# Splitting the raw down weights for the first fold stage, two heads without partial sums, and earlier maxima and gain loads

## The reference, cut to what matters

```python
h = _layernorm(x) * (1 + ca) + sa
scores = einsum('bqhd,bkd->bhqk', q, k) / HEAD_DIM ** 0.5      # causal
attn = softmax(scores)
x = x + ga * (einsum('bhqk,bkd->bqhd', attn, v) @ o_w.T + o_b)
h = _layernorm(x) * (1 + cb) + sb
y = fwht(h * SU_ug) / SCALE
y = silu(y @ W_gate.T * ws_gate) * (y @ W_up.T * ws_up)
y = fwht(y * SU_dp) / SCALE
x = x + gb * (y @ W_down.T * ws_down)
```

## Time and profile before

| | us |
|---|---|
| median of the runs | 1907.4 (1904.89 to 1908.88) |
| the profiled execution | 1910.14 |
| its span, first to last instruction | 1907.9 |
| PE busy | 1853.8 (97%) |
| DVE busy | 1368.3 (72%) |
| ACT busy | 848.6 (44%) |
| GpSimd busy | 555.2 (29%) |

### The profile page before, as it was taken

The page is one execution under the profiler, slowest core; times in us unless marked ns, Lnnn a source line. Parts: engine busy times, 40 slices in busy tenths (PEclk is TensorE's granted clock), DMA queues, the critical chain, the costliest instruction groups (busy, mean ns, idle before and its releaser), DMA issues.

```text
span 1907.9 us, 37938 instructions
## 1 busy us (share of the span) xinstructions
PE 1853.8 (97%) x14016; PEld 1554.0 (81%) x14016; DVE 1368.3 (72%) x3223; ACT 848.6 (44%) x1591; POOL 555.2 (29%) x653
## 2 busy tenths in 40 slices
PE   6999999999999999889999999999999999999998
PEld 3677777777777777668887889999999999999997
DVE  4788887878787777845558886776777666767655
ACT  4368655766576645642224433323323333333221
POOL 2367676667665655640100010100100100001000
PEclk8799999999999999989999999999999999999999
DMA  7433334343435778444459887888797787888884
GB/s 235 135 103 80 107 101 119 93 108 99 127 85 148 220 231 286 149 166 162 143 197 372 327 328 286 298 322 314 291 348 285 290 335 284 310 325 298 322 301 166
DMA packets 118702, 424.47 MB, mean 222 GB/s; under 512 B 26348, under 2 KB 39916, under 8 KB 104312
## 3 DMA queue, kind: packets, MB, share of 16 engines
q1 hardware_dynamic: 106856, 363.27, 55.9%
q10 hardware_dynamic: 11664, 58.79, 8.2%
HBM read 322.36 MB, written 65.29 MB: 203 GB/s over the span
## 4 chain that ended last, share of the span: by engine, by line
PE 47%; DVE 5%; ACT 2%; issue 1%; DMA 1%; POOL 1%; SPq 1%; DVEq 0%; ACTq 0%; POOLq 0%
PE banks L1822 23%; PE banks L1912 15%; PE banks L1691 7%; DVE ln_stats L1265 1%; POOL probs L1120 1%; PE banks L1788 1%; PE banks L1782 1%; DMA upgate_items_dram<-items_ring 1%; DVE x_normed L1277 1%; PE banks L1990 1%; DVE y L1390 0%; DMA upgate_raw<-in_w_ug 0%; ACT silu_gate L919 0%; ACT y_split L904 0%; ACT silu_gate L954 0%
## 5 line engine op out<-in xcount | busy, mean ns | idle before, releaser
L1120 POOL TENSOR_TENSOR probs<-probs 128x512 f32<-128x512 f32 x256 | 340.4, 1330 | 181.7 <-ACT probs L1015 160.5
L1912 PE MATMUL banks<-d_ring,y_split 128*128 128x512 f32 x1536 | 377.4, 392 | 1.9 <-DVE y_split L1410 1.9
L1015 ACT ACTIVATE probs<-banks 128x512 f32<-128x512 f32 x576 | 310.1, 596 | 103.3 <-PE banks L1958 100.0
L1912 PEld LDWEIGHTS banks<-d_ring,y_split 128*128 128x128 f32 x1536 | 281.7, 188 | 56.8 <-DVE y_split L1410 2.1
L1822 PE MATMUL banks<-h_t_split,items_ring 128*128 128x256 f32 x2280 | 321.0, 283 | 2.0 <-DVE both L1367 2.0
L1822 PEld LDWEIGHTS banks<-h_t_split,items_ring 128*128 128x128 f32 x2280 | 299.0, 191 | 13.8 <-ACT h_t L830 4.0
L1958 PE MATMUL banks<-q_stacks,k_stack 98*128 98x512 f32 (+3 forms) x768 | 250.8, 369 | 8.5 <-DMA q_stacks<-neg_max_rows 6.0
L1745 PE MATMUL banks<-k_stack,q_stacks 96*128 96x512 f32 (+3 forms) x768 | 249.9, 369 | 7.0 <-DMA q_stacks<-q_split 2.6
L1822 PE MATMUL banks<-input_sums,items_ring 128*128 128x256 f32 x1710 | 236.2, 283 | 0.0
L1149 POOL TENSOR_TENSOR x_normed<-h_t 128x512 f32<-128x512 f32 x6 | 7.9, 1309 | 775.6 <-ACT h_t L837 775.6
L1822 PEld LDWEIGHTS banks<-input_sums,items_ring 128*128 128x128 f32 x1710 | 218.9, 192 | 0.0
(11 more groups left out here) (180 smaller groups left out, 2612.7 us busy)
## 6 DMA issues: line engine op xcount, KB each, us to landing
items_ring<-upgate_items_dram SPq DMA_DIRECT2D x94, 1792.0 KB, 7.3
d_ring<-down_split_dram SPq DMA_DIRECT2D x128, 512.0 KB, 8.1
q_stacks<-q_split SPq DMA_DIRECT2D x192, 128.0 KB, 2.8
upgate_raw<-in_w_ug SPq DMA_DIRECT2D x32, 512.0 KB, 4.4
upgate_items_dram<-items_ring ACTq DMA_DIRECT2D x8, 1792.0 KB, 7.2
upgate_items_dram<-items_made ACTq DMA_DIRECT2D x8, 1792.0 KB, 6.8
x<-in_x SPq DMA_DIRECT2D x32, 256.0 KB, 2.9
o_group<-o_and_sums SPq DMA_DIRECT2D x256, 32.0 KB
```

The source lines that it names most:

```text
L1015: nc.scalar.activation(pr[:, probs_slot(H, u), :], score_bank[:, at % SLOTS_SCORE, :], ACT.Exp, scale=SCALE).then_inc(exped, 1)
L1120: nc.gpsimd.tensor_tensor(into, into if i else pr[:, probs_slot(H, u - 1), :], pr[:, probs_slot(H, u), :], ALU.add).then_inc(summed, 1)
L1912: last = nc.tensor.matmul(acc[:, t, :], ys[s][:, a, t * P:(t + 1) * P], dr[g % D_RING][:, m, :], start=(f == 0 and a + m == 0), stop=(f == ...
```

## The change

1. **Split raw weights.** ACT rounds a raw down-weight tile to float32r (`raw_high`), DVE takes the rest (`raw_rest`), into a new buffer `fold_raw_split` of two tiles, and the across tile becomes two float32r matmuls. Both are made two across tiles ahead, right behind the split of a tile's product; the first two in H = 46 behind units 0 and 2. The matrix `across` is copied once to float32r.
2. **Places of the across tiles.** Three in H = 48 (units 4, 7, 8) and in H = 52, none in H = 53. The first two along tiles are loaded five units before H = 54 starts, and no more one (`LOAD_BEFORE`).
3. **Two heads without added tiles.** In H = 62 and 63 GpSimd adds nothing, and PE multiplies every probability tile by ones (`WEIGHED_UNSUMMED`).
4. **Maxima of head 1.** Slots 0 to 2 stand before the turn of head 0's maxima, slots 3 to 5 behind the turn of the values, all ahead of head 0's first score; six fewer stand in head 0.
5. **Gains and residuals.** `load_gains` and two `load_residual` of the last batch move from behind the last head into SP's H = 61.
6. **Second block's input.** It is loaded in step 2 of the network, and no more in step 1.
7. Three semaphores of the start become one.

```diff
-FOLDS = [("across", left, u) for left, us in [(left, (4, 8)) for left in range(18, 11, -1)] + [(11, (1, 4))] for u in us]
+FOLDS = [("across", left, u) for left in range(18, 11, -1) for u in ((4, 7, 8) if left in (16, 12) else (4, 8))]
+FIRST_SPLITS = {(18, 0): 0, (18, 2): 1}
-STORE_AFTER, LOAD_BEFORE, FIRST_LOADS = 1, 1, 4
+STORE_AFTER, LOAD_BEFORE, FIRST_LOADS = 1, 5, 4
...
+            def raw_high(i):
+                if i == 0:
+                    act.wait_ge(across_in, 16)
+                    nc.scalar.activation(across[:], across_raw, ACT.Copy)
+                act.wait_ge(fold_in[i % FOLD_RING], 16 * (i // FOLD_RING + 1))
+                nc.scalar.activation(raw_split[:, i % 2, 0, :], raw[:, i % FOLD_RING, :], ACT.Copy).then_inc(raw_hi, 1)
...
                     nc.scalar.activation(fold[:, i % 2, 0, :], side[:, r, :], ACT.Copy).then_inc(fold_hi, 1)
+                    if i + 2 < FT:
+                        raw_high(i + 2)
...
+            def raw_rest(i):
+                dve.wait_ge(raw_hi, i + 1)
+                nc.vector.tensor_tensor(raw_split[:, i % 2, 1, :], raw[:, i % FOLD_RING, :], raw_split[:, i % 2, 0, :].bitcast(F32), ALU.subtract).then_inc(raw_lo, 1)
...
                     nc.vector.tensor_tensor(lo, side[:, r, :], hi.bitcast(F32), ALU.subtract).then_inc(side_free[r], 1)
+                    if i + 2 < FT:
+                        raw_rest(i + 2)
...
-                    pe.wait_ge(across_in, 16)
-                    pe.wait_ge(fold_in[i % FOLD_RING], 16 * (i // FOLD_RING + 1))
+                    pe.wait_ge(raw_lo, i + 1)
                     r = side_slot(key)
-                    last = nc.tensor.matmul(side[:, r, :], across[:], raw[:, i % FOLD_RING, :], start=True, stop=True)
+                    for m in range(2):
+                        last = nc.tensor.matmul(side[:, r, :], across[:], raw_split[:, i % 2, m, :], start=m == 0, stop=m == 1)
...
-                    if u in SUMMED_UNITS:
+                    if u in SUMMED_UNITS and H < ALL - UNSUMMED_HEADS:
                         add_unit(H, u)
...
-    return order + [("max", 0, i) for i in range(NS)] + [("top", 0), ("v", 0)]
+    order += [("max", 0, i) for i in range(NS)] + [("max", 1, i) for i in range(AHEAD_OF_TOP)] + [("top", 0), ("v", 0)]
+    return order + [("max", 1, i) for i in range(AHEAD_OF_TOP, EARLY_MAXIMA)]
...
+                if left == TAIL_IN:
+                    load_gains(B - 1)
+                    for t in range(2):
+                        load_residual(B - 1, t)
```

More of the change, by code:

```diff
@@ L94 @@
 FIRST_TOP_UNIT = 6
+AHEAD_OF_TOP, EARLY_MAXIMA = 3, 6
 SHIFTS_STEP, SHIFTS_UNIT = 1, 4
@@ L174, in side_work @@
     if H == 0:
-        for place, key in enumerate([("max", 1, i) for i in range(NS)] + [("max", 2, i) for i in range(NS)]):
+        for place, key in enumerate([("max", 1, i) for i in range(EARLY_MAXIMA, NS)] + [("max", 2, i) for i in range(NS)]):
             units[place // 2].append(key)
@@ L270, in program @@
                 x1xr=place(s, "x1_and_residual", [P, 4, D]), ga=place(s, "gain_row", [P, D]),
-                ob=place(s, "output_bias", [P, D]), across=place(s, "across", [P, P]),
+                ob=place(s, "output_bias", [P, D]), across=place(s, "across", [P, P], F32R),
                 kvb=place(s, "kvb", [P, 1]), qb=place(s, "qb_group", [P, 1]),
@@ L281, in program @@
                 W["raw"] = place(first, "fold_raw", [P, FOLD_RING, D])
+                W["raw_split"] = place(first, "fold_raw_split", [P, 2, 2, D], F32R)
             W["again"] = place(s, "fold_again", [P, AGAIN_RING, 2, D], F32R)
@@ L378, in phase @@
     x1, xr = x1xr[:, 0:2, :], x1xr[:, 2:4, :]
-    raw, fold, again, across = W["raw"], W["fold"], W["again"], W["across"]
+    raw, raw_split, fold, again, across = W["raw"], W["raw_split"], W["fold"], W["again"], W["across"]
     fx1, xn, hs, hb, fht = F["x1"], F["xn"], F["hs"], F["hb"], F["ht"]
@@ L387, in lent @@
         return buffer[:, first:first + k * n].rearrange("p (k n) -> p k n", k=k)
+    across_raw = fold[:, 1, 1, 0:P].bitcast(F32)
     q_raw, q_split, ow_raw = x1xr[:], Z["q_split"], Z["ow_raw"]
@@ L618, in network @@
                     load_items(g + HALVES_RING - FIRST_HALVES)
-                if f == X_STEP:
+                if f == (X_STEP if blk else FIRST_X_STEP):
                     if blk:
@@ L726, in _ @@
             load_down(2)
-            load_gains(B - 1)
-            for t in range(2):
-                load_residual(B - 1, t)
             for n in range(2):
@@ L783, in load_fold @@
                     if i == 0:
-                        act.dma_start(across[:], io["across"]).then_inc(across_in, 16)
+                        act.dma_start(across_raw, io["across"]).then_inc(across_in, 16)
                     act.dma_start(raw[:, i % FOLD_RING, :], io["w_down"].rearrange("(q j) n -> j q n", j=FT)[i]).then_inc(fold_in[i % FOLD_RING], 16)
@@ L1028, in step @@
                     left = ALL - H
+                    if (left, u) in FIRST_SPLITS:
+                        raw_high(FIRST_SPLITS[left, u])
                     if left == CROSS_LEFT and u == 6:
@@ L1565, in step @@
                     left = ALL - H
+                    if (left, u) in FIRST_SPLITS:
+                        raw_rest(FIRST_SPLITS[left, u])
                     if left == STAT_LEFT and 3 <= u < 3 + NT:
@@ L1980, in weigh @@
                     pe.wait_ge(masked, (H + 1) * len(TRIANGLES))
-                    pe.wait_ge(summed, (H + 1) * len(SUMMED_UNITS))
-                begun, last_of = set(range(PAIRS)) if part else set(), {row: i for i, (row, _, _) in enumerate(WEIGHED[part])}
-                for i, (row, kt, of) in enumerate(WEIGHED[part]):
+                    if H < ALL - UNSUMMED_HEADS:
+                        pe.wait_ge(summed, (H + 1) * len(SUMMED_UNITS))
+                products = (WEIGHED if H < ALL - UNSUMMED_HEADS else WEIGHED_UNSUMMED)[part]
+                begun, last_of = set(range(PAIRS)) if part else set(), {row: i for i, (row, _, _) in enumerate(products)}
+                for i, (row, kt, of) in enumerate(products):
                     if kt == "sum":
```

35 lines of the change are left out of this document (25 added, 10 removed).

## The result

| | before | changed |
|---|---|---|
| median, us | 1907.4 (1903.3 to 1908.9, 5 runs) | 1895.1 (1892.8 to 1899.0, 5 runs) |
| ratio | | 0.9936, interval 0.9919 to 0.9952 |
| the profiled execution | 1910.1 | 1895.1 |
| its span | 1907.9 | 1893.3 |
| PE busy | 1853.8 | 1846.4 |

The changed kernel is faster by 12 us, between the forecast (1899.1) and rival (a) (1893.1), and inside the range. It also lies just inside the forecast's own band, which began at 1894.5. All eleven runs of the changed kernel together have a median of 1894.9.

What follows compares the result with a forecast made beforehand. PE was taken to bound the attention, with DVE becoming the bound of heads 46 to 52. Terms -0.3 - 1.6 - 1.3 - 3.6 - 1.55 = -8.35 us, from median 1907.4, gave 1899.1 us; range 1890.5 to 1907.5.

Steps and rivals of the forecast that it cites:

- rival (a): Heads 46 to 52: no waiting for GpSimd, PE stays the bound; -14.3 us in all, 1893.1 us; chance 18%.
- the forecast's own band: Whole kernel: 1894.5 to 1903.5 us, the span given to the forecast itself, chance 50%.
- First fold stage: Heads 46 to 53: PE saves work on across tiles but DVE becomes the bound of heads 46 to 52; -0.3 us.
- The term of `raw_rest`: DVE, heads 46 to 52: each raw_rest costs 0.62 plus 0.36 us of waiting, 0.98; 16 cost 15.7 us.
- an operation that comes at a random time: First fold stage: raw_rest meets GpSimd's work by chance, waiting 0.33 us for adds and about 0.03 for masks.
- Rival (c): First fold stage: DVE waits for GpSimd at most raw_rest, 1.17 us each; +4.6 us, 1912.0 us; chance 9%.
- Second fold stage: First along tile, head 54: earlier stores and loads remove PE's wait of 1.58 us; -1.6 us.
- Start: Ahead of head 0: six maxima of head 1 fill PE's idle time; -1.3 us, bounds 0 and -3.5.
- if the clock rises when it does now: Start, head 0: with the half clock lasting until near 76 us as before, work done by then counts; -1.3 us.
- Last heads: Heads 62 and 63: GpSimd's waits go, head 63's maxima come later; -3.6 us, between 0 and -6.
- Rival (b): Last head: its maxima come only at 822.8; +2.7 us and not -3.6, 1905.4 us; chance 15%.
- First network steps: Network step 3: up and gate weights issued 2.72 us earlier, so the 1.55 us wait goes; -1.55 us.

Runs made afterwards that it cites:

- the kernel with both corrections: Changed kernel with raw_rest behind unit 8 issued three maxima later and gains and residuals loaded a head later; 1887.9 us, ratio 0.9893 to the kernel before.
- the changed kernel (again): The changed kernel, unchanged, run and profiled a second time beside the experiments; median 1894.0 us, ratio 0.9924 to the kernel before.

## Why the prediction was right, and where its size was off

**First fold stage** (-0.3; the trace says -1.1, twice): right in mechanism and nearly in size. Heads 47, 50 and 51 take 10.1 us (10.11, 10.12 and 10.10), where I had put 9.9 to 10.1, and head 53 takes 16.48 for 16.5. Head 46 was to be over 10.83 and is 10.64. The term of `raw_rest` was too high: 0.87 us in the mean over the 16, not 0.98. Its plain time is 0.68 and not the 0.62 that I took, and its wait 0.19 and not 0.36. The step that failed there is "an operation that comes at a random time": the order is the same in each head, so the one behind unit 8 meets the add in five of six heads (1.26 or 1.27 us), and the one behind unit 4 once in seven, for 0.08. DVE's terms fit less well than their sum: I had put 80.5 us of work and 1.5 of idle time in heads 46 to 52, and 75.8 and 4.5 were measured. Too much was put for `raw_rest` by 1.8 us, and another 3.2 (a part of the outputs, `o_group` and `o_split`) fell into head 53. That the idle time was put 3.0 too low, which hides most of that, is luck. Rival (a) is wrong for this kernel, and its 9.2 us for head 47 come out in the one with the rests moved (9.26). Rival (c) is wrong.

**Second fold stage** (-1.6; -1.8): right, and 1.41 us come back with the late issue.

**Start** (-1.3; about -3.6): the step that failed is "if the clock rises when it does now". The clock rises earlier, by 3 to 7 us of low clock according to the pair of executions (lengths times twice the missing share of PEclk: 20.4 and 16.9 us before, 13.7 and 13.6 now). I had that as the end of the range (-3.5), and it was the mean. This is the greater part of the 4 us between forecast and result.

**Last heads** (-3.6; -3.5 in the pair of profiles): right point by point. The maxima were to be issued at 812.4 and the first score to start at 816.1 less what was gained before (8.2 us at head 62), that is 804.2 and 807.9; it was 803.4 and 808.25. The low clock behind it was there, and the network was to start at 831.64 - 3.6 - 8.2 = 819.9; it started at 819.94. Part of this is luck: in five other kernels with the same last heads it was 24.5 to 25.6 us from head 62 to the network and not 23.4, a gain of 1.1 to 2.3. What differed is the clock behind the wait for the maxima: it was at the lower level for 3.4 us in both profiles of the changed kernel and for 6.8 in those five, the longer stretch that the prediction allowed for with -2.6. Rival (b), maxima as late as 822.8, is out.

**First network steps** (-1.55; -2.5 in the first pair, -4.8 in the second): the wait is gone, as forecast. The term was small because it counted the wait alone. One profile had shown a small wait, 1.55, where the next showed 2.30; behind that one the clock fell (0.57 from 855.64 to 859.60), as it did behind the 2.63 of the loads behind the last head, and not behind the 1.55. And the start of the network lay in a stretch of low clock before: its first 48 products took 11.82 us and take 11.18, which is 0.64 us.

**Sum.** With each stage as a mean over all profiles that have it in the one form and in the other: -3.6 (start), -1.1 (fold stage), -2.1 (head 54 to 58), -2.3 (last heads), -3.1 (network to product 400), in all -12.1 before rounding, and the medians say -12. The last heads were put 1.3 too high and the other four terms too low: with the last heads right, the total would have been 5 us off and not 4. My sum was -8.35. The rest (head 58 to 62: 46.8 in the mean of three against 45.7 of eleven) is within the chance of that stage. I had set the profiled execution 2.7 us above the median; by the later medians of the kernel before (1906.0, 1906.2 and 1907.4) it was 2.7 to 4.1.

A misjudgement that the sum doesn't show: I took DVE's load as the bound of the fold stage, where 3.0 us of `raw_rest`'s 13.9 were waiting, 2.3 of which a place three maxima on avoids, and the 3.2 us at head 63 as given with the change.

## What to carry to other kernels

Before work goes to an engine that shares a port, look at what the other engine does at that very instruction, head by head: in a fixed order the wait came at the same instruction in head after head, and a few places on it was gone or short. In the order of one queue, put bulk loads behind the small load that the next matmul waits for. And judge a change of 1% by stages that repeat and by medians, not by two profiles, which here differed by 14.6 and 20.4 us for a gain of 12.

## What the runs showed of the hardware

- A DVE `tensor_tensor` with both inputs in SBUF waited for a GpSimd add of two SBUF tiles that had started first: 1.26 and 1.27 us and not 0.68, in the same places of five heads, and 0.70 to 0.76 once it stood beside a mask. Where it waited, it ended 0.53 to 0.56 us behind the end of the GpSimd instruction, and so did the `o_split` of the earlier trace rows (677.31 against 676.75, where I had put 0.62). The waiting goes both ways: an add that started at 596.13, beside a `raw_rest` of 595.81, took 1.51 us and not 1.28. Nor does it need two inputs: the negation of the maxima, a `tensor_scalar` of 128x8 with one tensor input, took 1.15 us at 668.87 and 0.67 at 623.68, beside adds that ran until 669.99 and 624.33, and 0.18 at 602.04. This lock on a whole instruction is what the Trainium skill calls an exclusive lock ("SBUF — State Buffer", SBUF: two separate sides), and the trace agrees with it. In its "Advanced Engine Details and Errata", the section VectorE Performance Modes names two-port modes alone as blocking and gives `tensor_tensor` none; it doesn't say that nothing else waits, and read that way, as I did in the prediction, the measurement decides against it.
- The granted clock is not a property of the kernel alone. The same program was at the lower level for most of 68 to 76 us in one execution (0.55) and for a third of it in the next (0.82), and head 2 started at 89.0 and 86.8. Nor does the sum of PE's idle time tell it: from head 58 to head 62 the kernel with both corrections had 1.00 with 4.3 us idle, the changed kernel (again) 0.96 with 3.0.
- A megabyte read from DRAM (the first block's input) took 7.5 and 9.9 us from issue to landing in two executions of the kernel before, and 11.7 and 8.0 in two of the changed one. A wait for it that stands in one profile may be gone in the next, as DVE's 3.62 us were.
